# First attention of a two-layer network: a third query tile turned by VectorE

## The reference

```
Q1, Q2 = halves of xn @ Wq[h] + bq      K1, K2 = halves of xn @ Wk[h] + bk
A1 = Q1 K1^T / 8        A2 = Q2 K2^T / 8          # 1024 x 1024, per head and batch
P  = softmax(A1) - lam * softmax(A2)
O  = P @ (xn @ Wv[h] + bv)
x  = x + 0.2 * layernorm(concat(O) @ Wo + bo)
```

## Time and profile before

| | PE | PEld | DVE | ACT | POOL |
|---|---|---|---|---|---|
| busy us over the span | 1439.6 | 588.5 | 1376.4 | 1198.3 | 1003.8 |
| share | 92% | 37% | 88% | 76% | 64% |
| share of the chain that ended last | 53% | | 13% | 14% | 7% |

### The profile page before, as it was taken

The page is one execution under the profiler, slowest core; times in us unless marked ns, Lnnn a source line. Parts: engine busy times, 40 slices in busy tenths (PEclk is TensorE's granted clock), DMA queues, the critical chain, the costliest instruction groups (busy, mean ns, idle before and its releaser), DMA issues.

```text
span 1572.0 us, 28031 instructions
## 1 busy us (share of the span) xinstructions
PE 1439.6 (92%) x10243; PEld 588.5 (37%) x10243; DVE 1376.4 (88%) x2107; ACT 1198.3 (76%) x1911; POOL 1003.8 (64%) x727
## 2 busy tenths in 40 slices
PE   5899999999999999999999999986685999999985
PEld 1434443344434443344334433434541222222223
DVE  6798998999899989999999989988687999999947
ACT  4787888888888888888888888874342888888882
POOL 2999998898898988989889889880032011111112
PEclk9999999999999999999999999997696999999997
DMA  4243433343244323433343333420000110000001
GB/s 126 76 105 92 106 86 82 102 112 90 78 103 110 96 77 104 109 92 85 91 107 105 83 91 93 114 68 1 1 22 21 31 35 15 16 16 16 16 16 34
DMA packets 154641, 110.80 MB, mean 70 GB/s; under 512 B 31381, under 2 KB 142906, under 8 KB 154506
## 3 DMA queue, kind: packets, MB, share of 16 engines
q1 hardware_dynamic: 154378, 108.99, 26.5%
q0 software_dynamic: 128, 0.03, 0.0%
HBM read 53.82 MB, written 34.87 MB: 56 GB/s over the span
## 4 chain that ended last, share of the span: by engine, by line
PE 53%; ACT 14%; DVE 13%; issue 11%; POOL 7%; DMA 1%; SPq 0%; POOLq 0%; ACTq 0%; DVEq 0%
PE PS L1573 14%; PE PS L1585 10%; PE PS L1599 9%; ACT ering L847 7%; PE PS L1980 4%; POOL ering L656 3%; DVE nmx L1152 2%; PE PS L1942 2%; DVE region L1172 2%; PE PS L1632 2%; PE PS L1964 2%; ACT region L871 2%; DVE mxp L1479 2%; ACT ering L1059 2%; POOL ering L655 2%
## 5 line engine op out<-in xcount | busy, mean ns | idle before, releaser
L1152 DVE TENSOR_REDUCE nmx<-PS 128x1 f32<-128x1024 f32 x512 | 620.1, 1216 | 54.4 <-PE PS L1574 53.5
L847 ACT ACTIVATE ering<-PS,nmx 128x1024 f32<-128x1024 f32 x512 | 570.6, 1116 | 109.6 <-DVE nmx L1152 109.5
L656 POOL TENSOR_TENSOR ering<-ering 128x1024 f32<-128x1024 f32 x256 | 604.2, 2360 | 21.4
L1573 PE MATMUL PS<-region 64*128 64x512 f16 x1536 | 405.1, 381 | 20.4 <-ACT ering L847 14.5
L1574 PE MATMUL PS<-region 64*128 64x512 f16 x1536 | 405.2, 381 | 0.0
L655 POOL TENSOR_SCALAR ering<-ering,rho 128x1024 f32<-128x1024 f32 x256 | 287.3, 1122 | 95.2 <-DVE rho L1161 94.5
L1479 DVE TENSOR_REDUCE mxp<-PS 128x2 f32<-128x1024 f32 x256 | 304.2, 1222 | 34.3 <-PE PS L1964 29.9
L1059 ACT ACTIVATE ering<-PS 128x1024 f32<-128x1024 f32 x256 | 259.6, 1024 | 70.0 <-PE PS L1942 64.1
L1585 PE MATMUL PS<-ident,ering 128*128 128x128 f32 x1536 | 251.5, 286 | 15.6 <-ACT t L858 8.1
L1585 PEld LDWEIGHTS PS<-ident,ering 128*128 128x128 f32 x1536 | 161.6, 141 | 201.7 <-issue 73.8
L1573 PEld LDWEIGHTS PS<-region 64*128 64x128 f16 x1536 | 112.6, 94 | 261.3 <-ACT ering L847 110.2
(11 more groups left out here) (301 smaller groups left out, 1876.2 us busy)
## 6 DMA issues: line engine op xcount, KB each, us to landing
ptd<-t SPq DMA_DIRECT2D x256, 128.0 KB, 2.4
region<-region SPq DMA_DIRECT2D x64, 256.0 KB, 3.5
t<-ptd SPq DMA_DIRECT2D x44, 256.0 KB, 3.5
region<-ptd SPq DMA_DIRECT2D x44, 256.0 KB, 3.5
va<-ptd SPq DMA_DIRECT2D x20, 256.0 KB, 3.4
acc<-ptd SPq DMA_DIRECT2D x20, 256.0 KB, 3.5
osb<-scr SPq DMA_DIRECT2D x32, 128.0 KB, 3.3
rcp<-scr SPq DMA_DIRECT2D x32, 128.0 KB, 3.3
```

The lines of the kernel that those rows point to most:

```text
L656: P.tensor_tensor(e1, e1, e2, ALU.subtract).then_inc(s_sub_ok, 1)
L847: A.activation((E1, E2)[p][s % 4], PS[:, bank:bank + 2, :].rearrange("p a b -> p (a b)"), ACT.Exp, bias=nmx[:, 2 * s + p:2 * s + p + 1], s ...
L1152: V.tensor_reduce(nmx[:, 2 * s + p:2 * s + p + 1], PS[:, bank:bank + 2, :].rearrange("p a b -> p (a b)"), AX.X, ALU.max, negate=True).then ...
L1573: MM(PS[:, bank, :], top[0:64, ql, q], KT[b][0:64, p, kl, :], start=(j == 0), stop=(j == 2))
```

## The change

Tile 1 joins tiles 0 and 2 among those that DVE turns. The stages, their DRAM tensors and the load semaphores are now used in turn by a running count c = 3n + i of turned tiles, not by i and n. PV's pieces in steps 3 to 6 are 3, 2, 2, 1 and no longer 3, 1, 3, 1. Q's low part moves from the end of step 2 (behind v5's maximum) into step 3 (behind v6's maximum). ACT's wait for a free PT moves from the copy of tile 1 to that of tile 3.

```diff
-        BY_DVE = (0, 2)
+        BY_DVE = (0, 1, 2)
...
             def store_blocks(n, i):
-                sp.wait_ge(s_bt_ok, 2 * n + i + 1)
-                if n >= 1:
-                    sp.wait_ge(s_ptr_dma[(n - 1) % 2], 64 * ((n - 1) // 2 + 1))
+                c = len(BY_DVE) * n + i
+                sp.wait_ge(s_bt_ok, c + 1)
+                if c >= 2:
+                    sp.wait_ge(s_ptr_dma[c % 2], 32 * (c // 2))
...
             def load_turned(n, i):
-                sp.wait_ge(s_ptw_dma, 64 * (2 * n + i + 1))
+                c = len(BY_DVE) * n + i
+                sp.wait_ge(s_ptw_dma, 64 * (c + 1))
...
-                    store_blocks(n, 1)
-                    load_turned(n, 1)
+                    for i in range(1, len(BY_DVE)):
+                        store_blocks(n, i)
+                        load_turned(n, i)
...
-                if s in (1, 4) and i == 0:
+                if s in (3, 4) and i == 0:
                     at_least(act, s_pv_mm, n - 1 + half)
...
             def turn_blocks(n, i):
+                c = len(BY_DVE) * n + i
                 dve.wait_ge(s_sub_ok, 8 * n + BY_DVE[i] + 1)
-                if n == 0:
+                if c < 2:
                     dve.wait_ge(s_xt_mm, 4)
                 else:
-                    dve.wait_ge(s_ptw_dma, 64 * (2 * n + i - 1))
+                    dve.wait_ge(s_ptw_dma, 64 * (c - 1))
...
                     if own:
                         maximum(n, s, 0)
+                    if s == 3 and nxt and own:
+                        low_q(n + 1)
...
-                    if s == 2 and nxt and own:
-                        low_q(n + 1)
-                    if own and s in (3, 5):
-                        turn_blocks(n, s // 2 - 1)
+                    if own and s - 3 in BY_DVE:
+                        turn_blocks(n, BY_DVE.index(s - 3))
...
                 if j == 0:
-                    pe.wait_ge(s_ptr_dma[n % 2], 64 * (n // 2 + 1))
+                    c = len(BY_DVE) * n + len(BY_DVE) - 1
+                    for i in range(2):
+                        pe.wait_ge(s_ptr_dma[i], 32 * ((c - i) // 2 + 1))
...
-            PIECES = {3: (0, 1, 2), 4: (3,), 5: (4, 5, 6), 6: (7,)}
+            PIECES = {3: (0, 1, 2), 4: (3, 4), 5: (5, 6), 6: (7,)}
```

More of the change, by code:

```diff
@@ L465, in store_blocks @@
             def store_blocks(n, i):
-                sp.wait_ge(s_bt_ok, 2 * n + i + 1)
-                if n >= 1:
-                    sp.wait_ge(s_ptr_dma[(n - 1) % 2], 64 * ((n - 1) // 2 + 1))
+                c = len(BY_DVE) * n + i
+                sp.wait_ge(s_bt_ok, c + 1)
+                if c >= 2:
+                    sp.wait_ge(s_ptr_dma[c % 2], 32 * (c // 2))
                 for j in range(4):
-                    sp.dma_start(ptd[i].rearrange("(m p) (b c) -> p m b c", m=4, b=4)[:, :, j, :],
-                                 stage[i][32 * j:32 * j + 32, :].rearrange("p (m c) -> p m c", m=4)).then_inc(s_ptw_dma, 16)
+                    sp.dma_start(ptd[c % 2].rearrange("(m p) (b c) -> p m b c", m=4, b=4)[:, :, j, :],
+                                 stage[c % 2][32 * j:32 * j + 32, :].rearrange("p (m c) -> p m c", m=4)).then_inc(s_ptw_dma, 16)
             def load_turned(n, i):
-                sp.wait_ge(s_ptw_dma, 64 * (2 * n + i + 1))
+                c = len(BY_DVE) * n + i
+                sp.wait_ge(s_ptw_dma, 64 * (c + 1))
                 if n >= 2:
@@ L482, in load_turned @@
                 for k in range(2):
-                    sp.dma_start(PT[2 * n % 3][k][:, at:at + 4, :, :], ptd[i].rearrange(
-                        "p (b k c q) -> p b k c q", b=4, k=2, c=4)[:, :, k, :, :]).then_inc(s_ptr_dma[n % 2], 16)
+                    sp.dma_start(PT[2 * n % 3][k][:, at:at + 4, :, :], ptd[c % 2].rearrange(
+                        "p (b k c q) -> p b k c q", b=4, k=2, c=4)[:, :, k, :, :]).then_inc(s_ptr_dma[c % 2], 16)
             def swap_q(m):
@@ L843, in exponent @@
                     if tile in BY_DVE:
-                        act.wait_ge(s_bt_ok, 2 * prev + BY_DVE.index(tile) + 1)
+                        at_least(act, s_bt_ok, len(BY_DVE) * prev + BY_DVE.index(tile) + 1 if prev >= 0 else 0)
                     else:
@@ L1197, in turn_blocks @@
             def turn_blocks(n, i):
+                c = len(BY_DVE) * n + i
                 dve.wait_ge(s_sub_ok, 8 * n + BY_DVE[i] + 1)
-                if n == 0:
+                if c < 2:
                     dve.wait_ge(s_xt_mm, 4)
                 else:
-                    dve.wait_ge(s_ptw_dma, 64 * (2 * n + i - 1))
-                V.transpose(stage[i].rearrange("p (m k q) -> p k m q", m=4, k=8),
+                    dve.wait_ge(s_ptw_dma, 64 * (c - 1))
+                V.transpose(stage[c % 2].rearrange("p (m k q) -> p k m q", m=4, k=8),
                             E1[BY_DVE[i]].rearrange("p (k m q) -> p k m q", m=4, k=8)).then_inc(s_bt_ok, 1)
```

## The result

The kernel after takes 1584.11 us (1583.56 to 1585.17, four runs), the kernel before 1575.28 us in the same comparison: 8.8 us more, ratio 1.0063, 95% interval 1.0048 to 1.0078. The profiled executions stand 1583.56 to 1573.77, 9.8 us apart, and their spans 1581.7 to 1572.0, 9.7 apart. It is slower, as forecast, inside the range, and 3 us above the 1581 that I gave.

A forecast was written before the change was run, and what follows sets the result against it. PE paced v7 to the output product; DVE, with 0.40 us idle, would take over: +0.34 - 0.05 = +0.29 us an iteration. 7.8 + 0.8 - 1.0 - 1.0 + 0.4 = +7.0 us gave 1581 us, range 1574.5 to 1589.

The forecast's parts named there:

- DVE becomes the bound between v7 and v14: Plain iteration: with tile 1's turn added, DVE replaces PE as bound; v7 to v14 takes 13.51 us, before 12.75.
- 3.65 us from v14 to the turn of tile 5: Way from v14's maximum through exponential and output product to tile 5's turn, read from iteration 1 of the kernel before.
- the 3.50 of the other bound: Same way from v14 to tile 5's turn without iteration 1's slower passage; +0.14 us an iteration instead of +0.29.
- Steps 0 to 2 swallow nothing: From tile 5's turn to v7's scores stays 14.04 us, so a late v14 is passed on whole.
- Q's low part costs nothing and gives 0.05 us: Low part behind v6's maximum: no delay to v7's scores, cover 0.19 us; v7 comes 0.05 us sooner after them.
- The output product waits for ACT's exponential by 0.5 us and more: Sign that the forecast is right: this wait, 0.5 us and more, appears in each iteration.
- SP: nothing, with 5 us of cover: SP's added stores and loads per iteration cost nothing; tile 2's loads land 5 us ahead of their reader.
- The pieces do nothing: PV's pieces 3, 2, 2, 1: same work, moved within the stretch that DVE now bounds, so no cost or gain.
- Iteration 1: +0.8: Iteration 1 is late already with token weights filling 0.10 of DVE's idle; 1.16 - 0.30 - 0.05 comes on top, +0.8 us.
- DVE and POOL in each other's way: Rival: a block turn blocks POOL, whose 29.34 us grow by 1.24 to 30.6, still under 32.06; chance 1 in 100.
- Iterations 2 and 3: -1.0: POOL's extra work hides the 0.29 us; in iteration 3 PV's 0.99 us wait for DVE's constants goes, -1.0 us.
- The end: +0.4: End of the last iteration: adds 0.4 us to the whole.

The follow-up runs named there:

- tile_only: Kernel before with only the third tile turned by DVE, Q's low part and PV's pieces as before: 1583.69 us, ratio 1.0063 to the kernel before.
- lowq_pieces: Kernel after with only two tiles turned by DVE; Q's low part moved and PV's pieces 3, 2, 2, 1 kept: 1563.02 us, ratio 0.9924 to before.
- three_early_moved: Kernel after with tile 0's turn ahead of v7's maximum and the token weights moved to iteration 5: 1566.08 us, ratio 0.995 to before.
- weights_moved: Kernel after with DVE's token weights moved from step 5 of iteration 1 to step 3 of iteration 5: 1579.86 us, ratio 1.0034 to before.
- lowq_only: Kernel before with only Q's low part moved behind v6's maximum; two tiles and pieces 3, 1, 3, 1 stay: 1574.04 us, ratio 0.9996.
- pieces_only: Kernel before with only PV's pieces changed to 3, 2, 2, 1; two tiles, low part behind v5: 1574.36 us, ratio 1.0001.
- before_weights_first: Kernel before with the token weights ahead of iteration 1's second block turn, not behind it: 1575.57 us in a single execution.

## Why the prediction was right, and where it was off

The mechanism forecast for the plain iterations held, and so did its size. That the whole came within 3 us of the number is in part luck: iteration 1 was 4.4 us too low, and the rows from 4 to 31 and the end of the program were 2 us too high.

- *DVE becomes the bound between v7 and v14.* Right: 13.45 us for 13.51 forecast, no idle. Shown by the distances of tile_only, lowq_pieces and the kernel after (32.06, 31.30, 32.04) and by three_early_moved, where the same work in another place gives 31.50. Of my signs, PE's pauses ahead of v11 and v13 are there; ahead of v15 there is none to speak of.
- *3.65 us from v14 to the turn of tile 5*, taken from the one late iteration of the kernel before. Right: 3.68. With the 3.50 of the other bound, the forecast would have been 4 us too low in the plain iterations.
- *Steps 0 to 2 swallow nothing.* Right: 14.05 for 14.04.
- *Q's low part costs nothing and gives 0.05 us.* Right: 0.03 alone, and the stall came back ahead of v7.
- *The output product waits for ACT's exponential by 0.5 us and more* (one of my signs). Too big: its start is 0.48 us behind the last matmul's, 0.2 to 0.3 more than a matmul's step.
- *SP: nothing, with 5 us of cover.* Right: in iteration 14 of the kernel after tile 2's loads are issued at 522.47 and 523.03 and take 3.3 to 3.6 us to land in the median, their reader starts at 531.27, some 4.6 us after that, and from 180 us to 1040 PE waits for no DMA.
- *The pieces do nothing.* Right for the kernel after. But the reason that I gave hid that the same edit, with the low part moved and without the third tile, is worth 11.5 us. I priced each edit in the presence of the others and called it nothing; the change holds a gain of 11.5 us and a loss of 21.
- *Iteration 1: +0.8.* This is the term that was mis-sized: +5.2. Two steps in it failed. I took the token weights' length, 1.5 us, from the trace of before and held it fixed, though the change shifts DVE against POOL there; the two comparisons grew from 0.70 to 3.53 us (+2.8). I had weighed DVE and POOL in each other's way for the block turn, which keeps its length, and not for the comparisons, which don't. And I held the 3.65 us from v14 to the turn of tile 5 fixed for an iteration in which PE stands still for long; it became 5.31, since behind the wait of 4.20 us the granted clock was 0.50 (+1.6 to 1.7). With the comparisons off POOL's passes (weights_moved) both are gone. The runs do not show the lower clock without a long wait, nor the wait without the comparisons: it fell behind waits of 4.20, 3.54 and 2.99 us (after, tile_only, lowq_only), and stayed at 1.00 around those of 1.80 and 1.70 us at the same place in lowq_pieces and pieces_only.
- *Iterations 2 and 3: -1.0.* PV's wait of 0.99 us for the constants is gone, as forecast, and 2 to 3 gave 1.1, but 3 to 4 took 0.8 back. lowq_only shows the same pair (34.18 and 32.80), tile_only with the low part in its old place doesn't (35.1 and 32.05), so it comes with the low part's move. The timeline of PE ahead of v7 of iteration 4 shows what it waits for: the turn of a tile starts at 167.57 behind 0.72 us of waiting for POOL's pass (L659). The same wait is 0.99 us in lowq_only and 0.69 in weights_moved, 0.22 in the kernel before and absent in tile_only. So what PE gained in iteration 3 it lost to POOL, whose extra work bounds these iterations; I had used POOL to hide the 0.29 us and not the 1.0.
- *The end: +0.4.* The first exponential of the second attention comes 11.1 us later than before, which is 10.7 + 0.4 as forecast; the last one 10.8, and the end of the span 9.7. This last 1.4 us lies in stages that the change doesn't touch, and each of these figures is from one trace; runs of the kernel before differ by up to 7 us among themselves (1570.4 to 1577.1). The stretch from tile 0's last turn to the end also took 532.4 us in lowq_only and 533.2 in tile_only, against 535.3 before and 535.7 in pieces_only. What moves it is open.

## What to carry to other kernels

An engine that is 8% idle has no room if its idle time lies outside the stretch where the loop passes through it; count the pauses between the two events that the loop joins, and look first for another place in the list for the new work. When a change has several parts, price each also without the others: a good part can be hidden by one that makes another engine the bound. And a one-off piece of work in one iteration can be the largest single miss, if the change shifts it against another engine: here it cost more by itself (2.8 us), and then once more through PE, which had stood still and went on at half its clock (1.6 to 1.7 us).

## What the runs showed of the hardware

A comparison of 128 x 256 fp32 values from SBUF to SBUF on DVE takes 0.33 to 0.35 us with POOL idle (before_weights_first, weights_moved). Where a POOL pass over SBUF is under way or about to start, it lasts until 0.1 to 0.2 us behind that pass's end: 1.10 and 2.51 us were seen in the kernel after, 0.85 and 2.53 in lowq_only, 1.55 in before_weights_first. Beside the same passes the 128 x 1024 block turn (1.23 to 1.24 us), and maxima that read PSUM (1.2 us), keep their durations. POOL's passes keep their 1.12 and 2.36 us in all these cases; only in pieces_only and lowq_pieces, where a comparison of 0.31 us ran as POOL's short pass began, did that pass take 1.24 and 1.16 us.

PE's granted clock in iteration 1 of the kernel after was 0.50 from 92.00 to 98.00, in the second half of a wait of 4.20 us and in 4 us of work behind it. In tile_only, behind a wait of 3.54 us, it was 0.50 from 94.60 to 97.40, and in lowq_only, behind 2.99 us, from 98.00 to 100.50; there it fell only when PE was at work again. At 0.50 the eight matmuls of the V projection took 1.91 us in place of 1.13, and a unit's scores followed each other by 0.40 to 0.43 us in place of 0.22.
